# A mixer and experts layer on one core: when the slot fill and the experts' weights are loaded, and which engines do two pieces of the head

## The reference, cut to what matters

```python
x_norm = layer_norm(_ln_c(x), ln_g, ln_b)             # per token, 64 channels
xi, z = jnp.split(x_norm @ in_proj_w.T, 2, axis=-1)   # 128 inner channels each
u = jax.nn.silu(causal_conv4(xi) + conv_b)
dt, Bm, Cm = jnp.split(u @ x_proj_w.T, [4, 4 + 16], axis=-1)
delta = jax.nn.softplus(dt @ dt_proj_w.T + dt_proj_b)
# for each of 16 states n and each channel d, over 1024 tokens:
h = exp(delta * A[d, n]) * h + delta * u * Bm[:, n];   y += h * Cm[:, n]
y = (y + u * D) * silu(z) @ out_proj_w.T + skip_scale * x_norm
x = x + layer_norm(y, ln_g, ln_b) @ proj_w.T + proj_b
t = x + experts(layer_norm(x))      # buf[expert, position] = token, two matmuls, gather back
```

## Time and profile before

| | |
|---|---|
| median of 3 runs | 403.63 us (402.15 to 406.67) |
| profiled execution | 400.03 us |
| its span | 398.3 us |
| PE, DVE, ACT, POOL busy | 77%, 78%, 59%, 71% of the span |
| granted TensorE clock, mean | 0.88 of full |

### The profile page before, as it was taken

How to read it: one execution, slowest core, us unless ns; L and a number is a source line. 1 busy time by engine, 2 the same in 40 slices (tenths; PEclk the granted TensorE clock), 3 DMA queues, 4 the chain that set the end, 5 groups by cost and what they waited for, 6 DMA issues and landing times. The chain is left out here.

```text
span 398.3 us, 4350 instructions
## 1 busy us (share of the span) xinstructions
PE 306.8 (77%) x1257; PEld 180.7 (45%) x1257; DVE 308.8 (78%) x360; ACT 235.3 (59%) x519; POOL 281.8 (71%) x201
## 2 busy tenths in 40 slices
PE   7832978675996988589799769579879569999940
PEld 3311423222644343264434426346458446898940
DVE  4799995999899969878994789999998315667630
ACT  4456696723888595387849774746566135546320
POOL 3435845989696459989973999997688702477771
PEclk9965898989999799889869978999898859999975
DMA  5187999999688935858994366799931073000000
GB/s 102 31 278 258 265 270 343 416 216 381 256 281 285 363 122 183 316 194 275 320 322 166 111 235 208 268 305 365 288 84 31 15 199 79 4 16 18 21 12 0
DMA packets 43986, 78.68 MB, mean 198 GB/s; under 512 B 16050, under 2 KB 26093, under 8 KB 43962
## 3 DMA queue, kind: packets, MB, share of 16 engines
q1 hardware_dynamic: 41066, 73.88, 56.9%
q0 software_dynamic: 2896, 4.53, 4.1%
HBM read 72.30 MB, written 7.54 MB: 200 GB/s over the span
## 5 line engine op out<-in xcount | busy, mean ns | idle before, releaser
L509 POOL TENSOR_TENSOR prod<-h,csb 128x1024 f32<-128x1024 f32 (+1 forms) x64 | 143.9, 2254 | 34.4 <-DVE h L1305 12.4
L973 PE MATMUL Yp<-prod,ident 128*128 128x512 f32 (+1 forms) x256 | 127.6, 630 | 30.5 <-POOL prod L509 30.5
L1305 DVE TENSOR_TENSOR_SCAN h<-dA,Bp 128x1024 f32<-128x1024 f32 (+2 forms) x58 | 119.8, 2065 | 14.4 <-ACT dA L691 10.1
L973 PEld LDWEIGHTS Yp<-prod,ident 128*128 128x128 f32 x256 | 49.7, 207 | 91.5 <-issue 45.4
L1264 DVE TENSOR_TENSOR Bp<-Cp,bsb 128x1024 f32<-128x1024 f32 (+1 forms) x58 | 67.8, 1168 | 6.2 <-DMA bsb<-bc_rows 4.0
L691 ACT ACTIVATE dA<-delta,aneg 128x1024 f32<-128x1024 f32 (+1 forms) x58 | 62.9, 1095 | 12.7 <-DVE h L1305 8.3
L605 POOL DMA_INDIRECT out_dram<-dA,csb x30 | 30.0, 1002 | 28.3 <-DVE dA L1495 20.0
L548 POOL DMA_INDIRECT slots<-rows_,slot x30 | 30.2, 1005 | 6.6 <-issue 4.3
L1140 PE MATMUL Cp<-prod,w1s 128*128 128x384 f32 (+1 forms) x64 | 21.6, 462 | 0.0
L1154 PEld LDWEIGHTS Bp<-w2s,prod 128*128 128x128 f32 x152 | 18.1, 192 | 1.8 <-issue 0.3
L1481 DVE TENSOR_TENSOR dA<-Bp,b2s 128x320 f32<-128x320 f32 (+1 forms) x8 | 3.8, 475 | 19.2 <-PE Bp L1154 19.2
(11 more groups left out here) (289 smaller groups left out, 605.8 us busy)
## 6 DMA issues: line engine op xcount, KB each, us to landing
bsb<-bc_rows SPq DMA_DIRECT2D x48, 512.0 KB, 6.5
csb<-bc_rows SPq DMA_DIRECT2D x48, 512.0 KB, 5.8
bsb<-bc_rows SPq DMA_DIRECT2D x16, 384.0 KB, 5.9
csb<-bc_rows SPq DMA_DIRECT2D x16, 384.0 KB, 6.9
slots<-fill POOLq DMA_DIRECT2D x1, 2600.0 KB, 24.2
csb<-slots SPq DMA_DIRECT2D x6, 325.0 KB, 5.0
bcs<-bc_rows SPq DMA_DIRECT2D x2, 512.0 KB, 12.3
xs_in<-in_x_dram SPq DMA_DIRECT2D x1, 768.0 KB, 5.5
```

The lines of the kernel that those rows point to most:

```text
L509: po.tensor_tensor(prod[:, k % 4, c], h[:, k % 3, c], csb[:, k % CSLOTS, c], ALU.mult).then_inc(s_pP, 1)
L973: ins = te_.matmul(Yp[:, c], idn, prod[:, k % 4, c], start=False, stop=(n == 15), skip_group_check=True)
L1305: ins = ve.tensor_tensor_scan(h[:, k % 3, c], decays, drives, h[:, k % 3, c.start - 1:c.start] if i else 0.0, ALU.mult, ALU.add)
```

## The change

The fill moves from unit 0, after product 1, to unit 1, after product 1. `late()` moves from unit 0, n = 13, to unit 1, n = 6. In the head, ACT squares sequences 1 to 3 tile by tile with an accumulated sum (24 instructions of [128, 64]), 12 ahead of the first decay and 12 after the second; POOL's squares and DVE's sum are gone. POOL's scaling comes after product 0 instead of ahead of it. POOL's addition for the softplus is gone: PE adds `trel` and `ex` into `Yp` with four identity matmuls, and DVE's subtraction reads `Yp`. PE's first matmul of unit 0 into `Yp` waits for `f_delta`, that is for this subtraction.

```diff
@@ sync: units' loop
-                    if v == 0 and n == 13:
+                    if v == 1 and n == 6:
                         late()
@@ gpsimd
             rest = fz[:, 1:B].rearrange("p b t c -> p (b t) c")
-            pool.wait_ge(n_xm, 2)
-            po.tensor_tensor(squares[:, T:B * T, :], rest, rest, ALU.mult).then_inc(n_sq, 1)
-            pool.wait_ge(g_rel, 1)
-            pool.wait_ge(f_exp, 2)
-            po.tensor_tensor(trel[:, :], trel[:, :], ex[:, :], ALU.add).then_inc(f_high, 1)
-            pool.wait_ge(n_root, 1)
-            po.tensor_tensor(rest, rest, over(fs[:, 5, T:B * T], C), ALU.mult).then_inc(n_z, 1)
+            def scale_rest():
+                pool.wait_ge(n_root, 1)
+                po.tensor_tensor(rest, rest, over(fs[:, 5, T:B * T], C), ALU.mult).then_inc(n_z, 1)
...
                     scan(v, n)
-                    if v == 0 and n == 1:
+                    if v == 0 and n == 0:
+                        scale_rest()
+                    if v == 1 and n == 1:
                         pool.wait_ge(fill_done, 2)
                         po.dma_start(slots_dram.rearrange("(k p) r -> p k r", p=P), ...
@@ scalar
+            def square_rest(t0, t1):
+                for t in range(t0, t1):
+                    ins = ac.activation(squares[:, t, :], fz[:, t // T, t % T, :], ACT.Square, accum_out=fs[:, 2, t:t + 1])
+                ins.then_inc(n_sq, 1)
+            act.wait_ge(n_xm, 2)
+            square_rest(T, T + T * 3 // 2)
             act.drain()
             def other_roots():
...
-                act.wait_ge(n_var, 2)
+                square_rest(T + T * 3 // 2, B * T)
+                act.wait_ge(n_sq, 3)
@@ tensor: add_state, n == 0
                     pe.wait_ge(b_yg, v)
+                    pe.wait_ge(f_delta, 1)
@@ tensor: head
+            pe.wait_ge(g_rel, 1)
+            pe.wait_ge(f_exp, 2)
+            for q in range(2):
+                te_.matmul(Yp[:, HB[q]], idn, trel[:, HB[q]], start=True, stop=False)
+                ins = te_.matmul(Yp[:, HB[q]], idn, ex[:, HB[q]], start=False, stop=True)
+            ins.then_inc(f_high, 1)
             pe.wait_ge(w_fold, 1)
@@ vector: head
-            ve.tensor_tensor(at(delta, 0), trel[:, :], tabs[:, :], ALU.subtract).then_inc(f_delta, 1)
+            ve.tensor_tensor(at(delta, 0), Yp[:, :], tabs[:, :], ALU.subtract).then_inc(f_delta, 1)
...
-            dve.wait_ge(n_sq, 2)
-            ve.reduce_sum(fs[:, 2, T:B * T], squares[:, T:B * T, :], X).then_inc(n_var, 1)
```

## The result

The changed kernel took **410.12 us** in the median (4 runs, 408.91 to 412.64) against 403.25 for the kernel before beside it (4 runs, 402.15 to 406.67): ratio **1.0164**, 95% interval 1.0086 to 1.0242. Slower, by 6.9 us between the medians; forecast were 5.1. The profiled execution is the longest of the four, 412.64 us with a span of 410.8; the one profiled before (400.03) was shorter than any of the runs in its median, so the two traces lie 12.6 us apart and the medians 6.9. Some executions of a kernel run some per cent longer at a lower granted clock than the others: ratios leave them out, and a star in the table of the experiments marks a trace that was taken of one.

What follows compares the result with a forecast made beforehand. Row loads on DMA were taken as bound to 170 us, DVE within unit 0, a POOL chain through `f_ln` at its end. Terms -0.6 (unit 0) and +5.7 (unit 1) gave +5.1 on 403.63: 408.7 us, range 400 to 415.5.

Steps and rivals of the forecast that it cites:

- Head on DVE, 3.6 earlier: Head: DVE loses its sum of squares and a slow instruction; first scan 3.6 us earlier, at 29.4 instead of 32.97.
- The port rule: DVE in a two-port mode and POOL exclude each other for a whole instruction, so DVE's 2.72 us should fall to 0.68.
- Scaling 1.6 later: Unit 0: POOL's scaling of sequences 1 to 3 ends at 36.9 instead of 35.27, carrying 1.6 us to `f_ln`.
- Unit 0's end by POOL's chain, 0.6 gained: End of unit 0: with the fill gone, POOL's busy run from L514 brings `yt` only 0.6 us earlier, at 102.2.
- Unit 1, 5.7 lost: Unit 1: rows late behind the fill, then stopped 6.5 us by the late loads; `yt` 5.7 us late.
- my pattern: Unit 1: first row behind the fill lands 12.6 us after issue, the next 4.2, 4.0, 1.7 and 1.3 us later.
- rival 3: Unit 1: late loads run at the fill's half rate, 6.5 becomes 13; +11 us in all, 415; chance 0.14.
- Rival 1: Unit 1: late loads don't stack on the fill, nothing lost at `yt` on DVE's path; 403.2 us; chance 0.22.
- Rival 4: Unit 0: row waits stay because row loads alone fill the DMA engines; 0.6 falls to 0, 409; inside the forecast's range.
- Rival 2: End of unit 0: DVE sets it, `yt` gains 2.2 to 4 us; with rival 1 in unit 1, 399.1 us; chance 0.14.

Runs made afterwards that it cites:

- pe_add_only: Kernel before with only PE's addition from the new head; POOL's squares and DVE's sum kept, fill and late loads in unit 0; ratio 0.9947 to the kernel before.
- fill_split: Changed kernel with late loads back in unit 0 (n = 13) and the fill in unit 0 in four pieces; ratio 0.9947 to the kernel before.
- head_only: Changed kernel with fill and late loads both put back in unit 0, so only the new head remains; ratio 0.991 to the kernel before.
- fill_moved: Changed kernel with the late loads put back in unit 0 (n = 13), the fill staying in unit 1; ratio 0.9982 to the kernel before.
- late_n13: Changed kernel with the late loads at n = 13 of unit 1 instead of n = 6, the fill still in unit 1; ratio 1.003 to the kernel before.
- after_again: The changed kernel timed once more, nothing altered, beside other experiments on one chip; ratio 1.0177 to the kernel before.

## Why the prediction was right, point by point

The time (410.12; forecast 408.7, range 400 to 415.5), the side and the mechanism were right: rows late in unit 1, late loads on top of the fill, and a gain of the head that the chain to `f_ln` swallows. The size of unit 1 was not, and that the time came within 1.4 us of the forecast is partly luck.

- **Head on DVE, 3.6 earlier.** Right in kind: 2.72 became 0.69, PE's last record ended at 25.29 (25.2 forecast) and delta began at 25.93. The first scan was at 29.72 (29.4). The port rule that I named, of the Trainium skill (SBUF — State Buffer, Who interferes with whom), is borne out by pe_add_only, where POOL's squares stayed and only its addition was taken away: 0.69 instead of 2.72.
- **Scaling 1.6 later.** The squares were mis-sized: 12 take 2.9 us, not 2.4, for each pair of square and accumulator read comes 0.24 us after the last. It didn't matter: the root was done at 33.99, POOL with product 0 only at 34.5. The scaling ended at 37.2 (36.9), scan 3 waited for ACT and started at 42.85 (42.4), ACT's minus one ended at 74.45 (73.8).
- **Unit 0's end by POOL's chain, 0.6 gained.** Right in mechanism: L511 began at 74.53, right behind `f_ln`, and `yt` came 28.26 later, as before (28.45). The size was 0 instead of 0.6: `f_ln` came 2.3 later, not 1.6. In twelve of the fourteen traces the distance from this subtraction to `yt` is 28.0 to 28.5 (in fill_split with a piece of the fill, 1.0 us, in between). In head_only it is 27.1 and in fill_moved 26.5, and there PE was faster: its sum of a product near the unit's end took 1.98 us, at a granted clock of 1.00 in 96 to 101 us, against 2.71 before and 3.49 in the changed kernel, at 0.66 (before, after, head_only):

```profile
96.48 2.71 PE L973 MATMUL Yp<-prod,ident 128*128 128x512 f32 x4 [2.63 <-POOL prod L509]
...
96.49 3.49 PE L982 MATMUL Yp<-prod,ident 128*128 128x512 f32 x4 [2.62 <-POOL prod L506]
...
96.03 1.98 PE L982 MATMUL Yp<-prod,ident 128*128 128x512 f32 x4 [1.19 <-POOL prod L506]
```

  So I left out PE: the run of POOL that I took for solid ends in PE's sums, and their clock moves `yt(0)` by more than the 0.6 that I forecast. By my working the head alone could gain next to nothing. Of the 1.9 us by which head_only's `yt(0)` is earlier, 0.5 is L511's start (73.84), as I had it, and 1.4 lies behind it, where PE had its full clock.
- **Unit 1, 5.7 lost: the mis-sized term; 9.6 measured.** B row 6, which I put first behind the fill, landed at 114.4 after 4.1 us, untouched, not at 122.9. So the slow landings began one row later, and C5 (124.0 against 127.1) and B7 (128.3 against 131.1) came earlier than forecast, C6 (134.2 against 132.8) and B8 (136.7 against 134.1) later. The lateness of B8 is mostly the fill's own: it landed 22.7 us after its issue, where my pattern gives 20.1, and with no late loads behind it drive 8 found it 20.8 (late_n13) and 22.0 (fill_moved) after its issue. Then came the late loads, to which I gave the 6.5 us that they cost without the fill: between B8 and B9 lie 9.7 us, not 7.8. Of the 4.5 by which B9 was later than forecast, 2.6 are thus the fill's pattern and 1.9 the late loads. Drive 9 was 16.0 late, not 11.4. What it regained by `yt`, 6.4, was near my 5.7. This is the mechanism of rival 3, at a smaller price than its 11. There is also a slip in the sum: 11.4 less the waits of 1.95 and 2.03 is 7.4, not 7.9, which leads to 5.2 lost.
- **Units 2 and on, 0.** The profiled execution has 2.9 more there, in units 3 and 4. Its own time is 2.5 above its median, and unit 3 takes either 48.6 or 50.7 us in kernels with the loads left in unit 0 too (head_only and fill_split), so I don't read a cost into it.

Rival 1, that late loads don't stack on the fill, is out: late_n13 and after_again, timed side by side, differ in that alone, are 1.5% apart, and their intervals don't meet. Rival 4 is out, no row is waited for in unit 0. Rival 2's DVE-bound end didn't occur: DVE waits 2.70 for `yt`. The forecast of the time was closer than that of unit 1: by the traces 9.6 is lost there and 0 gained in unit 0, by the medians 6.9 in all. The ratio's interval allows 3.5 to 9.8 us, so the two can both hold. Which part of the difference is the executions' own isn't shown.

The best kernel found is head_only, 0.9% faster than before and about 2.6% faster than the change: take the head, leave the loads where they were. pe_add_only, with fewer edits, can't be told from it.

## What to carry to other kernels

A transfer that nobody waits for still has a price, paid by the transfers beside it. Two such transfers that were apart, put into one stretch, cost more than the sum of each one's move: 8.5 us at the end of unit 1, against 2.0 and none. Spreading the pieces within that stretch returned nothing that the times show; moving one past the other's landing returned 1.5%. Price a blocked issue by what lies ahead of it in the queue, not by the load in its row. Before counting a gain on a busy engine, find the engine that it waits for at the unit's end, and look whether the gain is still there one unit on.

## What was not expected of the hardware

- The time that SP needs to issue one DMA depends on the queue, not on it: the same 2 KB load was issued in 0.33 and in 19.44 us, a C row in 0.33 and in 11.86, and `b2s` in 7.15 to 9.39 with the weights and rows alone ahead of it, in 12.70 with one quarter of the fill issued before it and a second one during the hold, and in 21.81 with the whole of it. What fills up there (a count of descriptors or bytes) isn't told apart by these runs.
- Of two rows issued 0.36 us apart, both while POOL was issuing the fill (108.89 to 111.10), the first landed in 4.1 us and the second in 13.3.
- In unit 1 the DMA engines were 94% busy at 267 GB/s, and 71% busy at 252 GB/s without fill and weights: the busy share tells little of the bytes moved.
- TensorE's granted clock in unit 1 was 0.83 with PE waiting for late products and 0.93 before; in 30 to 45 us 0.50, the lower level (1.2 GHz), against 0.57 before. Whether this adds to the loss wasn't separated.
- The difference of 14 us between the groups of traces goes with TensorE's clock in the experts' part: 0.83 to 0.85 granted and 63 to 64 us of PE in before, after and late_spread, 0.72 to 0.78 and 73 to 81 us of PE in the eleven others.
